# A decoder layer on one core: score products in pairs on half the array's rows, three banks of scores, heads normalised per unit, and the second set's marks moved together

## The chip, the cores and the metric

The kernel runs on one core of a Trainium2 chip. The metric is the device time of one execution in microseconds. Lower is better. The engines are TensorE (PE, with its weight loads as PEld), VectorE (DVE), ScalarE (ACT), GpSimd (POOL) and SyncE (SP). Each has its own queue of instructions that it works through in order, and they meet through semaphores.

## The reference, cut to what matters

One decoder layer over x of 2 x 1024 tokens of 256 features, all in f32:

```python
x = layernorm(x + L0_attn(x))      # keys = h@Wk+bk, exp of key_att, cumsum over tokens, times values
x = layernorm(x + L0_xattn(x))     # 16 heads of 16 features over a context of 77 rows, masked softmax
x = layernorm(x + L0_ffn(x))       # 8 experts, 256 -> 1024 -> 256, the best 2 of each token, gelu
# inside L0_xattn:
scores = einsum('bhqd,bhkd->bhqk', Q, K) / sqrt(16);  scores = where(mask, -inf, scores)
attn_w = nan_to_num(softmax(scores));  merged = einsum('bhqk,bhkd->bhqd', attn_w, V) ...;  return merged @ W_o.T
# inside L0_ffn: logits = flat @ router_w.T + router_b; top_k of 2; softmax over the two; out += y_e * weight_e
```

## The kernel before

**Attention stage.** The 2048 tokens are 16 tiles of 128 tokens, 4 tiles to a chunk, 4 chunks. The cross-attention runs in 64 steps H, four to a tile; a step handles 4 heads (a quad). Two steps make a unit u = H // 2 of 8 heads. For a step TensorE multiplies the queries (features on the 128 rows, 16 to a head) with a block-diagonal table of keys `kbd` to 128x308 scores in a bank of psum_a and adds the mask with a second, bf16 product (`scores`, lines 1690 to 1714). The table holds zeros outside the 4 heads of a quad, so only 64 of the 128 rows of a product carry something: rows 0 to 63 in even steps, 64 to 127 in odd ones. VectorE takes the maximum (`maximum`, line 1212), ScalarE the four exponentials (`exponentials`, line 924), TensorE turns the probabilities (`turn_probs`, lines 1726 and 1731; two blocks of 128 in even steps into psum_c bank 0, three in odd steps into bank 1), ScalarE evicts them (`turned_probs`, line 937), and TensorE multiplies a unit with the values (`weigh_values`, line 1745, into psum_v). Per tile follow `normalise_heads` on VectorE (lines 1199 to 1205), `turn_heads` on TensorE (line 1755, into psum_m), its eviction (943), `project_out` (1763, psum_m), `residual` on VectorE (1174), `x2_invert` on GpSimd (607), `x2_normalise` on ScalarE (968), `output_features` (1679) and the router's logits (1686).

The order on each engine is written out by hand: a loop over H in each engine's program. In TensorE's step H come turn_probs(H), scores(H + 2), in even steps weigh_values(H/2 - 1), in steps 4t + 6 turn_heads(t), then pieces of the first attention for later chunks (`turn_attention` 1655, `x1_features` and `normalised` 1618, `keys`, `key_weights`, `queries`, `values` all 1611), and in steps 4t + 7 project_out(t). Scores of step H lie in bank H % 2 of psum_a. From step 50 on the routing of the first set (tiles 0 to 6) runs beside it: marks, a table of tokens, and from step 58 the gathers of token rows (`load_tile`, line 754).

**Expert stage.** Token rows are gathered into 39 tiles of 128; for each tile t TensorE runs `up(t)` (line 1860, 64 matmuls), the turn of the next tile's rows (`turn_rows(t + 1)`, 1800), and `down(t - 1)` (1885, 16 matmuls in either of two banks). ScalarE runs `hidden(t)` (gelu, 1041), `turned_rows(t + 1)` (953), `weighed_bias(t)` (1053), in this order; weighed_bias(t) waits for the variance that VectorE's sum_row(t - 2) makes, since it reuses its buffer. VectorE runs, per iteration t, inner_norm(t - 1), outer_norm(t - 2), indices(t + 2), weigh_output(t), add_input(t), sum_row(t), and GpSimd invert(t), load_base(t + 1), gathers of tiles ahead, add_bias(t + 1), store_tile(t - 1). sum_row(t) waits for the base rows that load_base(t) gathered.

The first seven tiles (FIRST = 7) hold only tokens of the first set. For the second set (tiles 7 and on) VectorE compares numbers into marks in three passes, `mark_positions(LAST)` and `mark_columns(LAST)` (line 1407, two instructions each) and `mark_tokens(LAST)` (line 1425, two). TensorE sums them (`mark_pairs(LAST)`, 1821), VectorE writes the table (line 1578), and `map_tiles(1)` and `load_tile(7)` on GpSimd follow.

## Time and profile before

| | us |
|---|---|
| three runs | 526.98, 528.07, 531.04 (median 528.07) |
| profiled execution: its own time | 529.84 |
| its span, first to last instruction | 528.1 |
| mean granted TensorE clock | 0.983 of full speed |
| busy: TensorE matmuls, weight loads | 492.8 (93%), 441.7 (84%) |
| busy: VectorE, ScalarE, GpSimd | 359.0 (68%), 266.5 (50%), 267.6 (51%) |

The span of 528.1 us is what the views below divide; the time of the same execution is 1.7 us longer. Busy times of matmuls overlap each other, because their ends are modelled, so what one costs is read from the distance between starts. An idle time in brackets stands before the instruction that ended it, with what it waited for.

### The profile page before, as it was taken

What the parts mean: (1) busy time and instruction counts of PE and PEld (TensorE: products, weight loads), DVE (VectorE), ACT (ScalarE), POOL (GpSimd) and SP (SyncE); (2) the same over time, 40 slices, a digit from 0 to 9 for tenths busy, and PEclk for the clock granted to TensorE, in tenths of its full rate; (3) what the DMA queues carried; (4) which work ended last, traced back from release to release, by engine and by line L of the source; (5) the groups of instructions that cost most, each with busy time, mean ns of one, the idle gap of its engine ahead of it and who ended that gap; (6) DMA issues with size and microseconds to landing.
All of it is one profiled execution on the core that took longest, in us unless ns stands there. A gap on an engine that the chain in (4) does not pass through costs nothing.

```text
span 528.1 us, 10924 instructions
## 1 busy us (share of the span) xinstructions
PE 492.8 (93%) x3286; PEld 441.7 (84%) x3286; DVE 359.0 (68%) x1035; ACT 266.5 (50%) x878; POOL 267.6 (51%) x407
## 2 busy tenths in 40 slices
PE   6879999989999899899949999999999999999991
PEld 6668877878888778899939999999999999999980
DVE  4878777767668885347965557765776566766675
ACT  3856677676867577552422344434444343444330
POOL 4342342223222524146666567775776576676555
PEclk9989999999999999999979999999999999999997
DMA  8049830745565736354374555665655666666420
GB/s 235 8 137 282 267 119 3 266 135 183 174 226 177 236 100 221 123 199 142 118 274 146 192 183 200 224 226 195 198 192 220 207 232 223 202 208 232 137 63 1
DMA packets 57536, 93.84 MB, mean 178 GB/s; under 512 B 12143, under 2 KB 49273, under 8 KB 52359
## 3 DMA queue, kind: packets, MB, share of 16 engines
q1 hardware_dynamic: 50231, 80.05, 44.7%
q0 software_dynamic: 5616, 12.82, 8.3%
q8 instruction: 28, 0.46, 0.4%
q10 hardware_dynamic: 1632, 0.27, 0.3%
q14 instruction: 29, 0.24, 0.1%
HBM read 65.64 MB, written 30.32 MB: 182 GB/s over the span
## 4 chain that ended last, share of the span: by engine, by line
PE 32%; issue 19%; DVE 18%; POOL 16%; DMA 9%; ACT 4%; POOLq 2%; SPq 0%; DVEq 0%; ACTq 0%
PE psum_b L1611 6%; PE psum_a L1710 4%; DMA work<-weighed_outputs,routing 4%; PE psum_v L1745 4%; POOL routing L809 4%; POOL out L813 3%; DMA front_then_w_ring<-token_rows,routing 3%; DMA weighed_outputs<-work 2%; POOL work L805 2%; DVE routing L1478 2%; PE psum_m L1763 2%; PE psum_m L1611 2%; POOL front_then_w_ring L754 2%; POOL work L800 2%; PE psum_a L1860 1%
## 5 line engine op out<-in xcount | busy, mean ns | idle before, releaser
L1041 ACT ACTIVATE front_then_w_ring<-psum_b,front_then_w_ring 128x128 f32<-128x128 f32 x160 | 45.5, 369 | 64.0 <-PE psum_b L1860 62.7
L1041 ACT ACTIVATE front_then_w_ring<-psum_a,front_then_w_ring 128x128 f32<-128x128 f32 x152 | 43.1, 369 | 65.4 <-PE psum_a L1860 65.4
L1860 PEld LDWEIGHTS psum_b<-front_then_w_ring 128*128 128x128 f32 x640 | 74.5, 192 | 1.4 <-issue 0.5
L1860 PE MATMUL psum_b<-front_then_w_ring 128*128 128x128 f32 x640 | 75.2, 275 | 0.1
L1885 PE MATMUL psum_v<-expert_w,front_then_w_ring 128*128 x320 | 72.5, 379 | 0.0
L924 ACT ACTIVATE work<-psum_a,score_max 128x77 f32<-128x77 f32 x256 | 62.2, 335 | 19.5 <-DVE score_max L1212 19.3
L1860 PEld LDWEIGHTS psum_a<-front_then_w_ring 128*128 128x128 f32 x608 | 70.9, 192 | 0.9
L1860 PE MATMUL psum_a<-front_then_w_ring 128*128 128x128 f32 x608 | 71.2, 275 | 0.0
L1885 PE MATMUL psum_c<-expert_w,front_then_w_ring 128*128 x304 | 70.6, 386 | 0.0
L1885 PEld LDWEIGHTS psum_v<-expert_w,front_then_w_ring 128*128 128x128 f32 x320 | 59.3, 190 | 7.3
L1885 PEld LDWEIGHTS psum_c<-expert_w,front_then_w_ring 128*128 128x128 f32 x304 | 57.3, 194 | 7.5 <-issue 0.3
L809 POOL TENSOR_TENSOR routing<-routing,minus_half 128x2 f32<-128x2 f32 x38 | 28.3, 744 | 58.5 <-DVE routing L1480 58.4
L800 POOL DMA_INDIRECT work<-weighed_outputs,routing x39 | 45.0, 1153 | 16.1 <-DMA weighed_outputs<-work 8.1
L1611 PE MATMUL psum_b<-front_then_w_ring,front_weights_then_tail 128*128 128x256 f32 (+1 forms) x216 | 49.0, 372 | 2.3 <-ACT front_then_w_ring L895 2.3
L813 POOL DMA_INDIRECT out<-work,routing x39 | 40.1, 1027 | 12.8 <-issue 8.2
L1611 PEld LDWEIGHTS psum_b<-front_then_w_ring,front_weights_then_tail 128*128 128x128 f32 x216 | 37.7, 190 | 8.7 <-ACT front_then_w_ring L895 3.5
L754 POOL DMA_INDIRECT front_then_w_ring<-token_rows,routing x39 | 38.1, 976 | 11.3 <-POOL routing L752 10.5
L1484 DVE TENSOR_TENSOR work<-work 128x256 f32<-128x256 f32 x38 | 16.5, 433 | 39.7 <-DMA work<-weighed_outputs,routing 39.2
L1745 PEld LDWEIGHTS psum_v<-front_weights_then_tail,work 128*128 128x128 f32 x320 | 39.2, 191 | 4.8 <-issue 4.8
L1212 DVE TENSOR_REDUCE score_max<-psum_a 128x4 f32<-128x308 f32 x64 | 30.1, 471 | 12.8 <-PE psum_a L1713 12.3
L1745 PE MATMUL psum_v<-front_weights_then_tail,work 128*128 128x51 f32 (+2 forms) x320 | 38.7, 268 | 0.0
L1492 DVE SCALAR_TENSOR_TENSOR work<-work,routing,front_weights_then_tail 128x256 f32<-128x256 f32 x39 | 18.9, 486 | 28.6 <-POOL routing L809 28.6
(257 smaller groups left out, 881.9 us busy)
## 6 DMA issues: line engine op xcount, KB each, us to landing
front_then_w_ring<-in_w1b SPq DMA_DIRECT2D x39, 1028.0 KB
weighed_outputs<-routing SPq DMA_DIRECT2D x16, 1024.0 KB, 6.3
expert_w<-in_w SPq DMA_DIRECT2D x8, 1024.0 KB, 10.6
weighed_outputs<-work SPq DMA_DIRECT2D x37, 128.0 KB, 2.2
token_rows<-front_then_w_ring SPq DMA_DIRECT2D x16, 128.0 KB
token_rows<-routing SPq DMA_DIRECT2D x1, 1152.0 KB, 5.4
second_buffers<-in_x SPq DMA_DIRECT2D x4, 256.0 KB, 4.8
front_weights_then_tail<-in_b SPq DMA_DIRECT2D x1, 1024.0 KB, 9.0
```

Source lines behind the costliest of these rows:

```text
L754: pool.indirect_dma_start(xt[t % ROWS], None, rows_dram, bass.IndirectOffsetOnAxis(load_of[:, t % ROWS:t % ROWS + 1], 0)).then_inc(xt_in[t ...
L800: pool.indirect_dma_start(base[t % 3], None, yw_dram[0:1 + YW_COLS * P, :], bass.IndirectOffsetOnAxis(row_idx[:, t % IDX, 0:1], 0)).then_i ...
L809: pool.tensor_tensor(rstd[:, t % 4], veps[:, t % 2], mhalf[:, 0:2], ALU.pow).then_inc(rstd_out, 1)
L813: pool.indirect_dma_start(out, bass.IndirectOffsetOnAxis(row_idx[:, t % IDX, 1:2], 0), u_rows[t % 3], None, bounds_check=T - 1, oob_is_err ...
L924: last = act.activation(prob[:, u % RING_U, at_k:at_k + SC], pa[:, H % 2, g * SC:(g + 1) * SC], ACT.Exp, bias=smax[:, j % 2, head:head + 1])
L1041: last = act.activation(hidT[t % 2][:, c, :], src[:, n, q * P:(q + 1) * P], ACT.Gelu, bias=bias[:, c:c + 1])
L1212: dve.tensor_reduce(smax[:, t % 2, quad * HG:(quad + 1) * HG], pa[:, H % 2, 0:HG * SC].rearrange("p (h k) -> p h k", h=HG), AX.X, ALU.max, ...
L1611: last = pe.matmul(dst[:, c, :], w[:, k, c * P:(c + 1) * P], src[:, k, :], start=(k == 0), stop=(k == KD - 1))
L1710: pe.matmul(dst, qT[it % 2][:, half, j * P:(j + 1) * P], kbd[:, it // CPB, half, g * HG:(g + 1) * HG, :].rearrange("p h k -> p (h k)"), st ...
L1745: last = pe.matmul(pv[:, half * width + v0:half * width + v1], probT[:, u % RING_U, c, :], vblk[:, t // (CPB * CT), half, c, v0:v1], start ...
L1860: last = pe.matmul(dst[:, n, q * P:(q + 1) * P], w1[:, k, c * P:(c + 1) * P], xtT[t % 2][:, k, :], start=(k == 0), stop=(k == KD - 1))
L1885: last = pe.matmul(y_psum(t), hidT[t % 2][:, c, :], w2_v[:, bass.ds(e, 1), c, :].rearrange("p a d -> p (a d)"), start=(c == 0), stop=(c == ...
```

## The change

Scores: psum_a gets a third bank, the one that was psum_m. The bank of a step is H % 2 in steps 0 to 5 and H % 3 from 6 on. Steps 0 and 1 and all steps from 8 on are multiplied in pairs, in the even step before: first both score products, each on only the 64 rows that carry something, then both masks. Steps 2 to 7 stay single and full.

Heads: the values of a unit of 8 heads go to psum_v columns 0 to 135 for every unit, and normalise_heads runs per unit. project_out writes columns 256 to 511 of the same bank. turn_heads writes psum_c bank 0, columns 256 to 511, except for the last tile; this bank also takes the turned probabilities of even steps, so turn_heads waits for their eviction. What used psum_m otherwise uses bank 2 of psum_a. residual, x2_invert and x2_normalise come one step later.

Expert stage: VectorE runs the three mark passes of the second set one behind the other, ahead of sum_row(0). later_map and the table come in iteration 2, ahead of sum_row(2). mark_pairs(LAST) on TensorE comes behind up(4) and not up(5). GpSimd runs rows_of_choice(1) ahead of its loop, map_tiles(1) and load_tile(7) at the start of iteration 2, and then load_tile(t + 5) in every iteration.

```diff
+PAIRED = 8
+def bank(H):
+    return H % 2 if H < PAIRED - 2 else H % 3
...
+        def heads_psum(t):
+            return pc[:, 0, D:2 * D] if t < TILES - 1 else pa[:, 2, 0:D]
+        def unit_psum():
+            return pv[:, 0:HALF * VW]
+        def output_psum():
+            return pv[:, D:2 * D]
...
 # GpSimd, H loop
-                if H % QUADS == 1 and H >= 9:
-                    x2_invert((H - 9) // QUADS)
+                if H % QUADS == 2 and H >= 10:
+                    x2_invert((H - 10) // QUADS)
...
 # GpSimd, expert loop
+            rows_of_choice(1)
             for t in range(LAST_TILE):
+                if t + AHEAD == FIRST:
+                    map_tiles(1)
+                    load_tile(FIRST)
                 invert(t)
...
-                if t == 0:
-                    rows_of_choice(1)
-                if t == 2:
-                    map_tiles(1)
-                for t_l in tiles_loaded_at(t):
-                    load_tile(t_l)
+                if FIRST < t + AHEAD < SLOT_TILES:
+                    load_tile(t + AHEAD)
...
 # ScalarE, H loop
-                if H % QUADS == 2 and H >= 10:
-                    x2_normalise((H - 10) // QUADS)
+                if H % QUADS == 3 and H >= 11:
+                    x2_normalise((H - 11) // QUADS)
...
 # VectorE, H loop
-                if quad == 2 and H >= 6:
-                    normalise_heads((H - 6) // QUADS)
-                if quad == 1 and H >= 9:
-                    residual((H - 9) // QUADS)
+                if H % 2 == 0 and H >= 4:
+                    normalise_heads((H - 4) // 2)
+                if quad == 2 and H >= 10:
+                    residual((H - 10) // QUADS)
...
 # VectorE, expert stage
             add_input(1)
+            mark_positions(LAST)
+            mark_columns(LAST)
+            mark_tokens(LAST)
             sum_row(0)
             indices(3)
-            mark_positions(LAST)
             row(inner_norm(0))
             sum_row(1)
-            mark_columns(LAST)
...
                 add_input(t)
-                sum_row(t)
                 if t == 2:
-                    mark_tokens(LAST)
                     later_map()
-                if t == FIRST - 4:
                     dve.wait_ge(pos_mm, LAST + 1)
                     dve.tensor_tensor(token_of[:, 0:P], table_psum(LAST), first_token_of, ALU.add).then_inc(table_ready, 1)
+                sum_row(t)
...
 # TensorE
+            def score_product(H, rows):
+                it, h = divmod(H, STEPS)
+                j, quad = divmod(h, QUADS)
+                half, g = divmod(quad, HC // HG)
+                pe.matmul(pa[:, bank(H), 0:HG * SC], qT[it % 2][rows, half, j * P:(j + 1) * P],
+                          kbd[rows, it // CPB, half, g * HG:(g + 1) * HG, :].rearrange("p h k -> p (h k)"), start=True, stop=False)
+            def score_pair(H):
+                before_scores(H)
+                before_scores(H + 1)
+                if H == PAIRED:
+                    pe.wait_ge(kexp_ready, 4)
+                if H >= PAIRED:
+                    pe.wait_ge(exp_ready, H - 1)
+                score_product(H, slice(0, HG * DK))
+                score_product(H + 1, slice(HG * DK, 2 * HG * DK))
+                add_mask(H)
+                add_mask(H + 1)
...
             def weigh_values(u):
-                if half == 0 and t >= 1:
-                    pe.wait_ge(merged_ready, t)
+                if u >= 1:
+                    pe.wait_ge(merged_ready, u)
+                if u >= 4 and half == 0:
+                    pe.wait_ge(r2_ready, t - 1)
...
             def turn_heads(t):
-                pe.wait_ge(merged_ready, t + 1)
+                pe.wait_ge(merged_ready, 2 * t + 2)
+                if t < TILES - 1:
+                    pe.wait_ge(pT_ready, t * QUADS + 7)
+                    if t >= 2:
+                        pe.wait_ge(x2T_ready, t - 1)
...
             def project_out(t):
                 pe.wait_ge(mT_ready, t + 1)
+                pe.wait_ge(merged_ready, min(2 * t + 3, 2 * TILES))
...
             def attention_step(H):
                 turn_probs(H)
-                if H + 2 < CHUNKS * STEPS:
+                if H + 2 < PAIRED:
                     scores(H + 2)
+                elif H % 2 == 0 and H + 2 < CHUNKS * STEPS:
+                    score_pair(H + 2)
...
-                if t == FIRST - 2:
+                if t == FIRST - 3:
                     mark_pairs(LAST)
```

## Rows read from the trace of the kernel before

**Rows 1.** Stretches, columns named in the first line: attention, the hole, the expert stage.
```profile
core 0: us, PE busy (x) PEld busy (x) DVE busy (x) ACT busy (x) POOL busy (x), PEclk, DMA share, GB/s
...
60.00:100.00 40.00, 39.02 (x246) 32.53 (x245) 30.49 (x82) 29.39 (x96) 15.36 (x42) 1.00 0.40 131
...
260.00:300.00 40.00, 32.90 (x215) 30.24 (x213) 23.91 (x73) 12.83 (x43) 22.84 (x31) 0.91 0.57 187
300.00:400.00 100.00, 100.00 (x695) 94.37 (x695) 66.16 (x194) 40.66 (x135) 67.87 (x84) 1.00 0.62 210
```

**Rows 2.** TensorE's timeline (start us, us, what) inside an attention step.
```profile
162.90 0.69 PE L1710 MATMUL psum_a<-front_weights_then_tail,front_then_w_ring 128*128 128x308 f32 x2
163.42 0.30 PE L1713 MATMUL psum_a<-identity_per_head,mask_bias 77*128 77x308 bf16 x1
163.56 1.89 PE L1611 MATMUL psum_b<-front_then_w_ring,front_weights_then_tail 128*128 128x256 f32 x8
```

**Rows 3.** Groups on tile psum_a: count, duration ns min/median/max, first and last start.
```profile
L1710 PEld LDWEIGHTS psum_a<-front_weights_then_tail,front_then_w_ring x64: 186/192/337, 25.4 to 174.0; 128*128 128x128 f32 x64
L1710 PE MATMUL psum_a<-front_weights_then_tail,front_then_w_ring x64: 422/425/721, 25.4 to 174.3; 128*128 128x308 f32 x64
```

**Rows 4.** Timeline of all engines around turn_heads of step 10.
```profile
65.18 0.42 PE L1755 MATMUL psum_m<-identity,work 128*128 128x128 f32 x2
...
66.55 0.94 ACT L924 ACTIVATE work<-psum_a,score_max 128x77 f32<-128x77 f32 x4
...
67.38 0.39 ACT L937 ACTIVATE work<-psum_c 128x256 f32<-128x256 f32 x1
...
67.55 0.55 PE L1731 MATMUL psum_c<-identity,work 128*128 128x128 f32 x3 [0.22 <-ACT work L924]
```

**Rows 5.** The same around turn_heads of step 62.
```profile
215.66 0.41 PE L1755 MATMUL psum_m<-identity,work 128*128 128x128 f32 x2
215.71 0.41 ACT L937 ACTIVATE work<-psum_c 128x256 f32<-128x256 f32 x1
```

**Rows 6.** VectorE groups by shape: normalise_heads (busy us, mean ns).
```profile
L1205 DVE TENSOR_TENSOR work<-psum_v,prob_scale 128x256 f32<-128x256 f32 x16 | 6.8, 425 | 0.6
...
L1199 DVE RECIPROCAL prob_sum_recip<-psum_v 128x16 f32<-128x16 f32 x16 | 4.0, 250 | 3.1 <-PE psum_v L1745 3.1
...
L1202 DVE SCALAR_TENSOR_TENSOR prob_scale<-score_max,prob_sum_recip 128x16 f32<-128x16 f32 x16 | 3.4, 211 | 0.5
```

**Rows 7.** TensorE's timeline: up(4), around down(4), and at the hole.
```profile
247.86 3.81 PE L1860 MATMUL psum_b<-front_then_w_ring 128*128 128x128 f32 x32
...
260.14 0.39 PE L1800 MATMUL psum_m<-identity,front_then_w_ring 128*128 128x128 f32 x2
260.36 3.62 PE L1885 MATMUL psum_v<-expert_w,front_then_w_ring 128*128 x16
...
274.66 0.69 PE L1800 MATMUL psum_m<-identity,front_then_w_ring 128*128 128x128 f32 x2 [7.10 <-DMA front_then_w_ring<-token_rows,routing]
275.22 5.19 PE L1885 MATMUL psum_c<-expert_w,front_then_w_ring 128*128 x16
```

**Rows 8.** VectorE's timeline: the first marks of the second set, and the table.
```profile
245.34 1.42 DVE L1407 TENSOR_TENSOR second_buffers<-routing 128x1152 f16<-128x1152 f16 x2
...
265.57 0.28 DVE L1578 TENSOR_TENSOR routing<-psum_c,routing 128x128 f32<-128x128 f32 x1
```

**Rows 9.** The chain of waits (start us, us, what): the gather of tile 7.
```profile
269.88 4.73 DMA front_then_w_ring<-token_rows,routing
```

**Rows 10.** ScalarE's timeline: weighed_bias(2) and turned_rows(4).
```profile
244.92 0.51 ACT L1053 ACTIVATE work<-front_weights_then_tail,routing 128x256 f32 x1 [6.61 <-DVE routing L1480]
...
247.34 0.43 ACT L953 ACTIVATE front_then_w_ring<-psum_m 128x256 f32<-128x256 f32 x1
```

**Rows 11.** Stretches again: the clock after sparse work.
```profile
24.00:27.00 3.00, 2.53 (x12) 1.80 (x12) 2.38 (x12) 0.85 (x3) 1.62 (x3) 0.78 0.16 15
27.00:30.00 3.00, 3.00 (x11) 2.24 (x11) 1.66 (x6) 0.97 (x4) 0.00 (x0) 0.66 0.12 14
```

More of the change, by code:

```diff
@@ L370, in decoder_layer @@
         v_rows = R[0:SC, 3840:3840 + B * D].rearrange("p (b u h d) -> p b u h d", b=B, u=2, h=HALF)
[L372 removed]
+        pa = ctx.enter_context(nc.psum_tensor("psum_a", [P, 3, 512], F32))
         pb = ctx.enter_context(nc.psum_tensor("psum_b", [P, KD, 512], F32))
@@ L923, in exponentials @@
                     at_k = (head % HALF) * SC
-                    last = act.activation(prob[:, u % RING_U, at_k:at_k + SC], pa[:, H % 2, g * SC:(g + 1) * SC], ACT.Exp,
+                    last = act.activation(prob[:, u % RING_U, at_k:at_k + SC], pa[:, bank(H), g * SC:(g + 1) * SC], ACT.Exp,
                                           bias=smax[:, j % 2, head:head + 1])
@@ L1688, in route_logits, with before_scores @@
                 last.then_inc(lg_mm, 1)
-            def scores(H):
-                it, h = divmod(H, STEPS)
-                j, quad = divmod(h, QUADS)
-                half, g = divmod(quad, HC // HG)
+            def before_scores(H):
                 if H == CPB * STEPS:
@@ L1739, in weigh_values @@
                     pe.wait_ge(own_made, 3 + 2 * B)
-                if half == 0 and t >= 1:
-                    pe.wait_ge(merged_ready, t)
-                width = HALF * VW
+                if u >= 1:
+                    pe.wait_ge(merged_ready, u)
+                if u >= 4 and half == 0:
+                    pe.wait_ge(r2_ready, t - 1)
+                if u == 2 * TILES - 1:
+                    pe.wait_ge(r2_ready, TILES - 1)
                 for c in range(BLOCKS):
-                    v0, v1 = (0, width) if c == 0 else (BLOCK_HEADS[c][0] * VW, (BLOCK_HEADS[c][-1] + 1) * VW)
-                    last = pe.matmul(pv[:, half * width + v0:half * width + v1], probT[:, u % RING_U, c, :],
+                    v0, v1 = (0, HALF * VW) if c == 0 else (BLOCK_HEADS[c][0] * VW, (BLOCK_HEADS[c][-1] + 1) * VW)
+                    last = pe.matmul(unit_psum()[:, v0:v1], probT[:, u % RING_U, c, :],
                                      vblk[:, t // (CPB * CT), half, c, v0:v1], start=(c == 0), stop=(c == BLOCKS - 1))
@@ L1762, in project_out @@
                 for k in range(KD):
-                    last = pe.matmul(pm[:, D:2 * D], mergedT[:, t % 2, k, :], wo_s[:, k, :], start=(k == 0), stop=(k == KD - 1))
+                    last = pe.matmul(output_psum(), mergedT[:, t % 2, k, :], wo_s[:, k, :], start=(k == 0), stop=(k == KD - 1))
                 last.then_inc(o_mm, 1)
@@ L1838, in _ @@
             queries(0)
-            scores(0)
-            scores(1)
+            score_pair(0)
             turn_attention(1)
```

74 lines of the change are left out of this document (33 added, 41 removed).

## The prediction

> **What bounds the kernel now.** I read the table of stretches first: which engine is full in which stage. In the attention stage (roughly 27 to 217 us) TensorE is busy for 39.0 of the 40 us shown, VectorE for 30.5 and ScalarE for 29.4 [rows 1]. In the expert stage TensorE is full, 100 of 100 us, except in one stretch, 260 to 300, where 7.1 us are missing and the granted clock averages 0.91 [rows 1]. So a microsecond of TensorE work removed from attention is worth up to a microsecond, and so is the hole at 267 us; work on the other engines counts only where TensorE waits for it. Second, TensorE's timeline inside a step, read by start times, since the busy times overlap: a score product of 128x308 in f32 is two matmuls that occupy the array for 0.52 us, and the next work starts 0.14 after the mask product [rows 2]. Third, the groups on psum_a: one score matmul lasts 425 ns while they start some 260 apart, so 0.16 us is the tail that an isolated one would show [rows 3]. Fourth, the hole: TensorE's timeline for its place, then VectorE's, ScalarE's and the chain of waits for its cause; their rows come with that step.
>
> **Score products in pairs.** Each of the 64 steps has two score matmuls, 128 in all (64 of them in the form shown, 64 in a twin form) [rows 3]. Now 29 pairs (steps 0 and 1, then 8 to 63) are issued as A1 A2 on rows 0 to 63, B1 B2 on rows 64 to 127. No row of this trace shows two matmuls on different halves, so I bound it. If nothing overlaps, the gain is 0. If both passes of B lie beside those of A, it is 2 x 0.26 = 0.52 a pair, 15.1 us in all. A1 and A2 need the same rows and stay serial; if the issue order is kept, only B1 can lie beside A2: three passes instead of four, 0.26 a pair, 29 x 0.26 = 7.5 us. I take this one. The Trainium skill, "TensorE: Matmul & The Clock Gate", Part 3, says that matmuls start and end in program order and that those of different row groups start about 4 ns apart; by that rule the saving is the same three passes. Going from 128 rows to 64 and back may cost something at each of 2 x 29 = 58 places. The nearest row is the 77-row mask product between full products: it starts 0.52 after the first score pass and the next work 0.14 later, so that change of rows costs nothing [rows 2]. I take 0 and keep as the upper end a switch that lets the array run empty and uncovers a load of weights (below). The even scores' mask now follows both products, some 0.26 to 0.52 us later; the maximum and the exponentials of that step have two steps to hide it. The odd scores come a step earlier, which only relieves VectorE and ScalarE.
>
> **Turned heads in another bank.** turn_heads (15 times in the loop) now writes the bank that holds the turned probabilities, so it waits until ScalarE has evicted those of the same step (line 937). That wait is new, and behind it on TensorE queue the pieces of the next chunk and the odd step's transposes and products. At step 10 TensorE turned the heads at 65.18, ScalarE finished the eviction at 67.38 + 0.39, and a signal takes some 0.06: 2.65 us late [rows 4]. At the last place, step 62, it is 0.52 [rows 5]. Over all 15 places the same subtraction gives 11 positive waits, these being the first and the last, 9.25 us together; that is the upper bound. Relief: at step 10 ScalarE's x2 normalisation stood ahead of the exponentials and held them back until 66.55, though their maximum was there near 65.0; it moves behind them, which makes 1.4 us [rows 4]. The pair puts some 0.4 us more product work between the even transposes and turn_heads, at each of the 11 waits; and at three of them TensorE idled anyway before the odd transposes, 0.22 at the one shown [rows 4], 1.65 together. 9.25 - 1.4 - 11 x 0.3 - 1.65 = 2.9; I take +3, with 0 and 9 as ends.
>
> **Smaller moves, each taken as 0.** Heads are normalised in 32 halves instead of 16 wholes: 16 x (0.25 + 0.21 + 0.42) = 14 us becomes, with nearly fixed reciprocals and a product of half the width, about 20 [rows 6]. VectorE's spare quarter of attention hides the 6 us; weigh_values now waits for the half before, but that is done right behind the maximum, ahead of the exponentials that TensorE needs first anyway. If VectorE were the bound, it would cost those 6. residual and x2_invert move one step later; the work is the same and its readers moved too. Before the first gather (load_tile(0)) they now stand in the same step, about 1.4 us more ahead of it, but the 1 MB bias load that competes with it moves behind it as well. TensorE idles 1.44 there today; -1.4 to +1.5, taken 0. project_out shares the bank with the units; its new wait is for work that follows a maximum issued two steps ahead: 0.
>
> **Second set's marks in a row.** Today TensorE ends up(6) at 267.5 and idles 7.10 until the rows of tile 7 land; then the clock is at its lower level (1.2 GHz): the turn takes 0.69 instead of 0.39, down(5) 5.19 instead of 3.62. Hole: 7.1 + 0.3 + 1.6 = 9.0 [rows 7]. The table is written at 265.57 + 0.28, the last act of iteration 3 [rows 8]; the gather behind it is issued at 269.88 and takes 4.73 [rows 9]. Now map and table stand in iteration 2. The price: three marks (1.42 us of busy time, 1.33 by their starts, 4.0 in all [rows 8]) stand ahead of sum_row(0). ScalarE's weighed_bias(2) waits for exactly that, already 6.61 us today, and hidden(3) and turned_rows(4) queue behind it; the turned rows end at 247.77 and up(4) starts at 247.86, without slack [rows 7, 10]. So a new hole of 4.0 us opens before up(4). Following it: up(4) at 251.9, table at about 262 (the base rows of tile 1, asked for 4 us later, hold VectorE), gather at 263.4, landed at 268.1; TensorE reaches tile 7 at 271.4. The old hole closes. In the 4.0 us the clock probably falls, too: after the sparse work near 24 us it was 0.78 and 0.66 for two stretches of 3 us, 3.4 us at the lower level [rows 11], worth up to 1.7. I take 1.6. Sum: -9.0 + 4.0 + 1.6 = -3.4; ends -5.1 (the clock stays) and 0 (tile 7 or the next two come late again, 3.4 us).
>
> **Sum.** -7.5 + 3.0 - 3.4 = -7.9 us. The profiled execution took 529.84 (span 528.1), 1.8 above the median of 528.07; against the median: **520.2 us**.
>
> **Rivals.**
> 1. *Switching rows costs more than the overlap gives (slower).* Place: the 58 borders in attention, on TensorE. If at each the array runs empty (425 - 260 = 0.16 us [rows 3]) and the next weights can't be loaded ahead (0.19 by the weight-load row [rows 3]), it is 58 x 0.35 = 20.5 us: 540.7. With the empty array alone, 9.4 us: 529.6. It decides from 7.9 / 58 = 0.14 us a border. For it: nothing in this trace has 64 rows, so nothing speaks against it but the mask's free border. The Trainium skill, "TensorEngine Tiling (Array Packing)", Key Properties, says that a change of tiling mode drains TensorE, and gives no price; no row here shows whether 77 rows count as another mode. Chance 0.18 for the cheap form, 0.14 for the dear one.
> 2. *No overlap at all*, the change doesn't do what it says: -7.9 + 7.5 = -0.4, 527.7. Every f32 matmul is already a pass of a full-width stream. Chance 0.12.
> 3. *Full overlap of both passes*: -15.5, 512.6. It needs B1 to start with A1. Chance 0.06.
> 4. *The wait for the eviction of the turned probabilities takes it back*: +9 instead of +3, and VectorE's 6 us partly with it: 526 to 529. For it: the attention stage leaves TensorE no slack, and the longest waits were VectorE's doing, which gets more work. Chance 0.10.
> The forecast has 0.40.
>
> **How the numbers follow.** About 1% (5.3 us) can be told from no change. Faster by more than that (below 522.8): forecast and rival 3, 0.46. Within 1%: the cheap form of 1 (0.18), 2 and 4, together 0.40, less 0.04 that may fall above 533.4: 0.36. Slower: 0.14 + 0.04 = 0.18. The range leaves out the dear switch (0.14) and the outer part of full overlap: 512.5 to 533. The forecast's own range, from its ends of the eviction wait, the hole and the gather: 516 to 528.
>
> **What would show it.** On TensorE the second product's first matmul starts within a few ns of the first product's second; from the first of the pair to the mask 0.78 us means three passes, 0.52 full overlap, 1.04 none. A gap before the pair and before the mask prices the border. turn_heads would wait for line 937's successor, 3 us in all. A wait of 4.0 us before up(4), none before tile 7, and the clock low once between 248 and 256. The forecast is wrong if attention is not 4 us shorter, or the stretch from down(2) to up(7) not 3 us shorter.

## The result: slower by 3.7 per cent, and the profile after

The changed kernel took **549.54 us** in the median (545.59 to 550.61, 4 runs), against 528.05 before; the ratio is 1.0368, interval 1.0314 to 1.0421. That is 19 us slower (21.5 by the medians), outside the range of 512.5 to 533 and on the other side of the forecast. The profiled execution has a span of 547.4 us, 19.3 more than before. Because the kernels of different groups below ran beside their own runs of the kernel before, I compare them by their ratios, and turn a ratio into microseconds with 528.

First the stretches, columns as in [rows 1].

```profile
core 0: us, PE busy (x) PEld busy (x) DVE busy (x) ACT busy (x) POOL busy (x), PEclk, DMA share, GB/s
60.00:100.00 40.00, 35.88 (x234) 28.84 (x234) 30.12 (x84) 28.54 (x92) 14.86 (x40) 1.00 0.31 98
...
190.00:220.00 30.00, 26.27 (x143) 19.94 (x143) 17.89 (x73) 17.60 (x63) 8.57 (x18) 0.78 0.50 179
...
300.00:400.00 100.00, 100.00 (x692) 94.43 (x692) 67.30 (x196) 42.08 (x141) 67.94 (x85) 1.00 0.62 210
```

The expert stage is as it was. In attention TensorE is busy for 35.9 of 40 us where it was 39.0 [rows 1], no other engine does more in the same time, and late in the stage the granted clock falls to 0.78. Attention lost more than the whole kernel did: the last projection starts at 248.3 us instead of 225.7, 22.6 later, and the expert stage gave 3.3 back.

Waiting is only a part of this. Of the 22.6 us, the waits that the profile lists (below) make 13.2. Over the same stretch, from 27 us to the last projection, TensorE's busy time rose too, from 188.9 to 197.5 us, although the pairs took work away, and the granted clock was 0.94 where it was 0.99. If TensorE had been bound by its clock all the time, that would be worth 0.05 x 221 = 11 us, an estimate from above.

The pair saves what was forecast, but not in the way that was forecast. TensorE's timeline in a step, as [rows 2]:

```profile
142.24 0.38 PE L1753 MATMUL psum_c<-identity,work 128*128 128x128 f32 x2
142.55 0.79 PE L1716 MATMUL psum_a<-front_weights_then_tail,front_then_w_ring 64*128 64x308 f32 x4
143.27 0.44 PE L1722 MATMUL psum_a<-identity_per_head,mask_bias 77*128 77x308 bf16 x2
143.55 1.10 PE L1775 MATMUL psum_v<-front_weights_then_tail,work 128*128 128x136 f32 x9
```

From the first product to the first mask 0.72 us (forecast 0.78 for three passes, 1.04 for none saved), and 1.00 to the next work. Two single products with their masks took 2 x (0.52 + 0.14) = 1.32 [rows 2]. But there are no three passes one behind the other. Two views of short windows, 142.5 to 142.6 and 143.1 to 143.2, part the four matmuls of that line into two and two:

```profile
142.55 0.53 PE L1716 MATMUL psum_a<-front_weights_then_tail,front_then_w_ring 64*128 64x308 f32 x2
...
142.92 0.43 PE L1716 MATMUL psum_a<-front_weights_then_tail,front_then_w_ring 64*128 64x308 f32 x2
```

Two matmuls start within 0.01 us of each other, the other two 0.36 later, again within 0.01, and the mask 0.36 behind those. The two passes of one product start some 0.26 apart in the kernel before [rows 3], so I read a couple as one pass of the even and one of the odd product, although no row names which. Then both passes lie side by side, as rival 3 had it, but a couple takes 0.36 us instead of 0.26; why, no run shows.

The same place with full rows (e2 below):

```profile
143.98 0.38 PE L1753 MATMUL psum_c<-identity,work 128*128 128x128 f32 x2
144.20 1.20 PE L1716 MATMUL psum_a<-front_weights_then_tail,front_then_w_ring 128*128 128x308 f32 x4
145.24 0.43 PE L1722 MATMUL psum_a<-identity_per_head,mask_bias 77*128 77x308 bf16 x2
```

Behind the same two transposes the half-row pair starts 0.31 us after them, the full-row pair 0.22: the border from 128 to 64 rows costs 0.09 us here, and 0.07 behind the router's logits (0.44 against 0.37), at nearly every pair of both kernels. From the transposes to the mask it is 1.03 against 1.26 us, from the logits to the mask 1.16 against 1.49. So the half rows save 0.23 us a pair in one half of the pairs and 0.33 in the other, about 7.5 us in the 28 pairs of the loop.

What TensorE waits for between 27 and 240 us (releaser, us in total, times, longest), before and after:

```profile
PE psum_c L1726 <- ACT work L924: 3.3, 3, 1.5
PE psum_c L1731 <- ACT work L924: 1.7, 3, 0.8
PE psum_b L1800 <- DMA front_then_w_ring<-token_rows,routing: 1.4, 1, 1.4
```

```profile
PE psum_c L1788 <- issue: 5.6, 6, 1.6
PE psum_b L1662 <- DVE front_then_w_ring L1157: 3.2, 3, 1.6
PE psum_b L1618 <- ACT front_then_w_ring L901: 2.3, 3, 1.6
PE psum_v L1797 <- ACT work L949: 2.1, 5, 0.9
PE psum_b L1618 <- ACT front_then_w_ring L888: 2.0, 4, 0.6
PE psum_c L1788 <- ACT work L943: 1.6, 1, 1.6
PE psum_c L1788 <- DVE work L1212: 1.3, 1, 1.3
```

All lines of these lists together are 9.8 us before and 23.0 after. The turned heads (L1788) wait for 8.5 of them, where they waited for none; 1.3 of the 8.5 are put down to VectorE's normalisation (L1212) and not to the eviction. "issue" stands where the profile names no single releaser; the timeline of all engines around one of these waits does (step 54, with the residual's sum first, and one pass of the first set's marks behind it):

```profile
212.03 0.41 DVE L1180 TENSOR_TENSOR front_then_w_ring<-psum_v,front_then_w_ring 128x256 f32<-128x256 f32 x1
...
213.22 1.15 DVE L1414 TENSOR_TENSOR front_weights_then_tail<-routing 128x896 f16<-128x896 f16 x2
214.29 0.47 DVE L1219 TENSOR_REDUCE score_max<-psum_a 128x4 f32<-128x308 f32 x1
...
214.80 0.97 ACT L930 ACTIVATE work<-psum_a,score_max 128x77 f32<-128x77 f32 x4 [2.57 <-DVE score_max L1219]
...
215.64 0.40 ACT L943 ACTIVATE work<-psum_c 128x256 f32<-128x256 f32 x1
...
216.14 0.41 PE L1788 MATMUL psum_c<-identity,work 128*128 128x128 f32 x2 [1.35 <-issue]
...
217.03 0.79 PE L1797 MATMUL psum_v<-front_weights_then_tail,work 128*128 128x256 f32 x1 [0.16 <-ACT work L949]
```

VectorE comes to the odd maximum at 214.29 only, behind the residual of the tile with its moments (0.8 us) and, at this place, 1.15 us of marks that the kernel before has too. ScalarE's exponentials wait for it, the eviction of the turned even probabilities stands behind them on ScalarE's queue, and the turned heads start 0.1 us after that eviction ends. It is the chain that the prediction named, at the upper end of its price.

The expert stage after, as [rows 7], down(2), up(4), the turn of tile 5 and down(3):

```profile
266.69 3.62 PE L1920 MATMUL psum_v<-expert_w,front_then_w_ring 128*128 x16
274.82 5.44 PE L1895 MATMUL psum_b<-front_then_w_ring 128*128 128x128 f32 x32 [4.51 <-issue]
...
281.10 0.39 PE L1836 MATMUL psum_a<-identity,front_then_w_ring 128*128 128x128 f32 x2
281.33 3.62 PE L1920 MATMUL psum_c<-expert_w,front_then_w_ring 128*128 x16
```

There is the new hole ahead of up(4), 4.51 us (forecast 4.0), and none of over 0.2 us behind it.

### The profile page after: what moved, and what is told of

Read it like the earlier page. It is cut to its first block, busy times and chain, and to the rows that moved or that the text cites. A ratio compares the mean times of both kernels' runs of the same rounds, so it can differ in the third digit from the quotient of the medians.

```text
span 547.4 us, 11002 instructions
## 1 busy us (share of the span) xinstructions
PE 500.5 (91%) x3286; PEld 441.9 (81%) x3286; DVE 365.0 (67%) x1083; ACT 267.2 (49%) x878; POOL 269.6 (49%) x407
## 4 chain that ended last, share of the span: by engine, by line
PE 33%; issue 19%; POOL 17%; DVE 14%; DMA 10%; ACT 5%; POOLq 1%; SPq 0%; DVEq 0%; ACTq 0%
DMA work<-weighed_outputs,routing 9%; PE psum_b L1618 8%; PE psum_v L1775 5%; POOL routing L815 4%; PE psum_a L1716 4%; POOL out L819 3%; POOL work L811 2%; PE psum_v L1797 2%; POOL work L806 2%; DVE routing L1485 2%; PE psum_a L1722 2%; PE psum_a L1618 2%; ACT work L930 2%; POOL front_then_w_ring L769 2%; DMA weighed_outputs<-work 1%
## 5 line engine op out<-in xcount | busy, mean ns | idle before, releaser
L1895 PE MATMUL psum_b<-front_then_w_ring 128*128 128x128 f32 x640 | 77.2, 280 | 4.5 <-issue 4.5
L1895 PEld LDWEIGHTS psum_b<-front_then_w_ring 128*128 128x128 f32 x640 | 76.7, 197 | 5.7 <-issue 4.9
L1920 PE MATMUL psum_c<-expert_w,front_then_w_ring 128*128 x304 | 69.0, 380 | 0.0
L1618 PE MATMUL psum_b<-front_then_w_ring,front_weights_then_tail 128*128 128x256 f32 (+1 forms) x216 | 52.5, 392 | 5.9 <-ACT front_then_w_ring L901 3.5
L1618 PEld LDWEIGHTS psum_b<-front_then_w_ring,front_weights_then_tail 128*128 128x128 f32 x216 | 40.0, 203 | 12.9 <-ACT front_then_w_ring L901 5.1
L1775 PEld LDWEIGHTS psum_v<-front_weights_then_tail,work 128*128 128x128 f32 x320 | 40.3, 196 | 1.9 <-ACT work L943 0.6
L622 POOL TENSOR_SCALAR routing<-routing 128x1 f32<-128x1 f32 x14 | 5.1, 361 | 71.7 <-DVE routing L1186 71.7
```

What stands on the lines that cost most here:

```text
L1618: last = pe.matmul(dst[:, c, :], w[:, k, c * P:(c + 1) * P], src[:, k, :], start=(k == 0), stop=(k == KD - 1))
L1775: last = pe.matmul(unit_psum()[:, v0:v1], probT[:, u % RING_U, c, :], vblk[:, t // (CPB * CT), half, c, v0:v1], start=(c == 0), stop=(c == ...
L1895: last = pe.matmul(dst[:, n, q * P:(q + 1) * P], w1[:, k, c * P:(c + 1) * P], xtT[t % 2][:, k, :], start=(k == 0), stop=(k == KD - 1))
L1920: last = pe.matmul(y_psum(t), hidT[t % 2][:, c, :], w2_v[:, bass.ds(e, 1), c, :].rearrange("p a d -> p (a d)"), start=(c == 0), stop=(c == ...
```

## The experiments

The theory after the result: the time is lost in attention to two handovers that lost their cover, the eviction ahead of the turned heads, and ScalarE's work between steps that have both score products and steps that have none. Rivals: the row halves (borders), the lower clock, VectorE's extra instructions.

| kernel | median us | ratio to before | interval |
|---|---|---|---|
| changed | 549.54 | 1.0368 | 1.0314 to 1.0421 |
| e1 expert edits alone | 527.05 | 0.9973 | 0.9951 to 0.9995 |
| e2 pairs, all 128 rows | 548.56 | 1.0393 | 1.0327 to 1.0459 |
| e3 single scores | 537.36 | 1.0177 | 1.0120 to 1.0233 |
| e4 e3, heads in their own bank | 528.98 | 1.0009 | 0.9982 to 1.0035 |
| e5 changed, eviction first | 540.64 | 1.0236 | 1.0183 to 1.0288 |
| e6 e5, projection later | 554.86 | 1.0551 | 1.0480 to 1.0622 |
| e7 e3, eviction first | 531.61 | 1.0060 | 1.0028 to 1.0093 |
| e8 e5, residual earlier | 545.06 | 1.0336 | 1.0291 to 1.0380 |
| e9 e5, pair in the odd step | 536.67 | 1.0143 | 1.0088 to 1.0199 |
| e10 e5, all 128 rows | 545.47 | 1.0305 | 1.0244 to 1.0367 |
| e11 e5, more products | 541.16 | 1.0227 | 1.0174 to 1.0279 |
| e12 e9, heads in the odd step | 537.16 | 1.0134 | 1.0100 to 1.0169 |
| e13 e1, one bias later | 526.38 | 0.9896 | 0.9856 to 0.9936 |
| e14 e1, all biases later | 524.89 | 0.9910 | 0.9875 to 0.9944 |

**Which part costs: e1 to e4.** e1 is the kernel before with the diff of the expert stage alone. e2:

```diff
-                score_product(H, slice(0, HG * DK))
-                score_product(H + 1, slice(HG * DK, 2 * HG * DK))
+                score_product(H, slice(0, P))
+                score_product(H + 1, slice(0, P))
```

e3 takes the changed kernel and issues scores(H + 2) in every step again, in bank H % 2; e4 moreover frees the heads:

```diff
-            return pc[:, 0, D:2 * D] if t < TILES - 1 else pa[:, 2, 0:D]
+            return pa[:, 2, 0:D]
...
-                    pe.wait_ge(pT_ready, t * QUADS + 7)
```

> The kernel before with only the expert-stage edits (marks in a row, table and first gather of the second set in iteration 2, mark_pairs behind up(4)). The prediction's term for it is -3.4 us: 524.6 against 528.0. If these edits carry part of the loss, it is above 528; if they carry more of a gain than the term, below 523.

> The changed kernel with the same pairs, banks and waits, but each score product of a pair over all 128 rows, so nothing can overlap. Theory (the waits on turned heads and on what follows them make the loss, the pairs do save 0.23 us each): about 6 us slower than the changed kernel, 556. Rival (going from 128 to 64 rows and back costs more than it gives, or the row halves disturb the neighbours): faster than the changed kernel, 535 to 545.

> The changed kernel with single, full scores in two banks issued each step as before; the heads still go to the bank of the turned probabilities with the wait for their eviction, normalised per unit, output product beside the units. Theory (that wait): as slow as the changed kernel or slower, 548 to 558. Rival (the pairing and its order, even scores later, is what starves VectorE and ScalarE): 526 to 532.

> As the single-score variant, but the turned heads go to a bank of their own and wait only for the merged heads, as before. It keeps the normalisation per unit, the output product in the units' bank, residual and x2 one step later, and the expert edits. Theory (the wait for the eviction): back to 524 to 530. Rival (the shared bank of units and output product, or the later residual, makes the loss): above 540.

The steps between them: expert edits -1.4 us; e4 over e1 +1.9 (normalisation in halves, the shared bank, the residual a step later; the intervals overlap, so it may be nothing); the turned heads in the shared bank with their wait for the eviction, e3 over e4, **+8.9**; both scores in the even step, with a third bank, e2 over e3, **+11.4**; the row halves, changed over e2, -1.3, within the intervals of each other. So the row halves are no loss, and the 7.5 us of work that they save buy next to nothing.

e4 came as expected and e1 between its term and no change. e2 and e3 fit neither of their cases: e2 was to be 6 us slower than the changed kernel and is not, and e3 lies between its ranges, since the wait and the pairing each carry about half of the loss.

Where did the saved 7.5 us go? Not into waits: those listed are 23.0 us in the changed kernel and 22.1 in e2. The granted clock differs: 0.94 in the changed kernel from 27 us to its last projection, 0.98 in e2, and over the whole span 0.960 to 0.972 in the four runs of the one, 0.973 to 0.981 in the four of the other. A clock lower by 0.04 over 220 us is worth up to 9 us, an estimate, which is about what the shorter products save. That TensorE is granted less because it has less to do fits this, and e11 below; no run shows it as the cause.

**The eviction wait alone: e5 and e7.** One order turned round on ScalarE, in pairs (e5) and with single scores (e7):

```diff
-                if H >= 2:
+                early = H % QUADS == 3 and H >= 7
+                if early:
+                    turned_probs(H - 1)
+                if H >= 2:
                     exponentials(H)
-                if H >= 1:
+                if H >= 1 and not early:
                     turned_probs(H - 1)
```

> The changed kernel with one order turned round on ScalarE: in the last step of each tile (4t+7) the eviction of the turned even probabilities (0.40 us) goes before the exponentials of the odd scores (0.97 us), not behind them. Theory handover: TensorE's turning of the heads waits for that eviction, which ScalarE gives only after exponentials that themselves wait for the odd maximum on VectorE; then the waits of the turned heads (7.2 us between 60 and 222 us, against nothing in the kernel before) shrink to under 1 us and the time falls by 6 to 9 us, to 541 to 543. Rival ScalarE: the exponentials start later by as much as the eviction comes earlier, the next turned odd probabilities are late by the same, and the time stays at 547 to 550. Rival order: the loss sits in the pair itself (both scores in the even step), then only 2 to 4 us come back.

> The kernel with single full-row scores (that of e3, 537.4 us) with the same turn of order on ScalarE as e5. Theory handover: the 8.4 us between e3 and e4 are this wait alone, and this kernel comes to 528.5 to 531. Rival ScalarE: 536 to 538, the wait only moves. Rival bank: the heads in the bank of the turned probabilities cost in other ways too, then 532 to 535.

-7.0 us in pairs, -6.2 with single scores: for the most part the turned heads waited for the order of two instructions on ScalarE. e7 ends at 531.6, just above the range of its theory and 2.7 us above e4 by the ratios; that rest of the shared bank's 8.9 us is not this order. With the wait nearly gone from both, pairs with full rows (e10, below) still stand 13 us above the single scores (e7).

**What is left of the pair's price: e6, e8, e9, e12.** e6 moves the projection to step 4t+8 behind the next pair; e8 moves the residual to step 4t+9 and lets the weighing wait for it; e9 moves the pair:

```diff
-                elif H % 2 == 0 and H + 2 < CHUNKS * STEPS:
+                elif H % 2 == 1 and H + 3 < CHUNKS * STEPS:
                     score_pair(H + 2)
```

(with logits and ranks a step later); e12 turns the heads behind turn_probs(4t+7), ahead of that pair, and has the old order on ScalarE.

> e5 and beside it the output projection of tile t in step 4t+8 behind the next pair of scores, not at the end of step 4t+7. Theory bare odd steps: with both score products in the even step, nothing stands between the turned heads and the projection in the odd step but the turned odd probabilities (0.5 us), and TensorE waits for ScalarE's copy of the turned heads (6.8 us in all in the full-row kernel with pairs, 0.4 us with single scores); with the pair (1.1 us) as cover these waits go and the kernel is 4 to 7 us faster than e5, 535 to 538. Rival: the projection is hidden behind ScalarE anyway and the time is that of e5 within 2 us. Rival later residual: the projection comes later, so the residual and the next weighing wait, and it is slower than e5 by 3 us or more.

> e5 and beside it the residual of tile t one step earlier on VectorE (step 4t+9, behind the odd maximum, where the kernel before has it), with the weighing of the next unit waiting for it. Theory odd maximum: the odd maximum stands behind normalisation and residual (1.3 us) on VectorE and the odd exponentials wait for it; freed of the residual the kernel is 2 to 5 us faster than e5, 537 to 541. Rival: the weighing (1.2 us) now waits for the residual on TensorE and the kernel is slower than e5 by 2 to 8 us, 545 to 550.

> e5 with the pair of score products moved from the even to the odd step: at odd step H the scores of H+2 and H+3 on the two row halves (steps up to 8 single, the last one single); the logits of a tile and the ranks go one step later, into the bank of an odd step. Theory bare odd steps: in e5 the even step holds pair (1.1 us), weighing (1.2 us) and turned heads, the odd step nothing but the turned probabilities and what waits for ScalarE (projection and pieces: 12 us of waits against 3 in e7); with pair and weighing in different steps the waits go and the kernel comes to 525 to 532, 9 to 15 us below e5. Rival early scores: what costs is that the even score of a pair is made late against its maximum and exponentials, whichever step it is in, or that queries are not ready a step earlier; then it stays at 538 to 545. Rival clock: the time follows the stretches at the lower clock; the granted clock of 60 to 222 us then tells more than the waits.

> e9 (pair in the odd step, 536.7 us) with the turned heads moved into the odd step too, behind the turned odd probabilities and ahead of the pair, and ScalarE's eviction back behind the exponentials. The odd step then holds turned probabilities 0.5, heads 0.4, pair 1.1 and projection 1.0, and the pair stands between heads and projection. Theory cover: neither the eviction nor the copy of the heads is waited for (3.1 us of waits in e9), 531 to 535. Rival balance: the even step has only 1.6 us of work and TensorE waits longer for the odd exponentials (5.9 us in e9), 537 to 541. If it is 535 to 537, both do and undo each other.

e6 and e8 went the way of a rival in time, but not for its reason: waits for the residual are 0.5 us in e6 and 0.7 in e8. e6 shows best what happened. TensorE's and ScalarE's timeline of it, from the odd step to the next even one:

```profile
205.29 0.49 PE L1761 MATMUL psum_c<-identity,work 128*128 128x128 f32 x3
205.49 0.39 ACT L949 ACTIVATE work<-psum_c 128x256 f32<-128x256 f32 x1 [1.21 <-PE psum_c L1791]
205.78 0.59 ACT L974 ACTIVATE front_then_w_ring<-front_then_w_ring,routing 128x256 f32<-128x256 f32 x1
206.26 0.96 ACT L930 ACTIVATE work<-psum_a,score_max 128x77 f32<-128x77 f32 x4
207.28 0.44 PE L1689 MATMUL psum_c<-identity,front_then_w_ring 128*128 128x128 f32 x2 [1.50 <-ACT work L930]
```

With the projection gone, the odd step has only its transposes (0.49 us) to cover 0.96 us of exponentials and the way there: ScalarE stood idle for 1.21 us until the heads were turned, copied them and normalised the tile, and only then came to the exponentials. TensorE waits for them, 13.3 us at 12 places, and e6 is 17 us slower than e5 (14 by the medians), far more than I had expected even on its rival's side. The bare step was real, but the projection had been its cover. In e8 the new waits are for the even exponentials (4.2 us at 3 places). It is 5 us slower, but all its listed waits together are no longer than those of e5 (18.7 and 19.3 us), so its cause stays open.

e9 puts the pair where nothing else stood. TensorE's waits between 27 and 240 us in e9:

```profile
PE psum_c L1762 <- ACT work L930: 5.9, 7, 1.9
PE psum_b L1665 <- DVE front_then_w_ring L1160: 2.7, 2, 1.9
PE psum_b L1840 <- DMA front_then_w_ring<-token_rows,routing: 1.9, 2, 1.1
```

The waits for the copy of the turned heads (1.3 us at 4 places in e5) and for the eviction in line 888 ahead of the pieces (2.0 us at 4 places) are gone; 4.9 us come back, half of what I expected, and the time lies between the ranges of theory and rival. In their place the odd transposes wait for their exponentials (5.9 us), since now the even step is the thin one. e12 moves 0.4 us of work more into the odd step: these waits grow to 8.6 us, the others shrink, and the time is the same. By the ratio (535.1 us) that is the third case of its expectation, by the median (537.16) the lower end of its rival's.

**Half rows once the wait is gone: e10.** e5 with the edit of e2.

> e5 with both products of a pair over all 128 rows (the zero rows too), as e2 is to the changed kernel. It costs TensorE 0.23 us in each of 28 pairs, 6.4 us of work. Theory cover: TensorE has waits of about 15 us between 27 and 240 us in e5 and takes the longer products in them; 540 to 543. Rival TensorE bound: 546 to 548, the half rows save their whole work once the eviction wait is gone.

3.6 us slower than e5 by the ratios (4.8 by the medians), between the two theories. The intervals overlap, so this is likely and not shown: the shorter products pay a part of what they save. What keeps the rest is again not the listed waits (19.3 us in e5, 19.7 in e10); the granted clock of 60 to 240 us is 0.95 in e5 and 0.98 in e10.

**The clock: e11.**

```diff
+                if H % QUADS == 3 and H >= 11:
+                    for _ in range(3):
+                        pe.matmul(pa[:, bank(H), 0:P], ident[:, :], ident[:, :], start=True, stop=True)
                 if H % QUADS == 3 and H >= 7:
                     project_out((H - 7) // QUADS)
```

> e5 with three more 128x128 products (about 0.2 us each at the higher clock, results thrown away) on TensorE ahead of each projection from tile 1 on, where TensorE waits for ScalarE's copy of the turned heads. 14 times 0.6 us is 8.4 us more work. Theory clock: the lower-clock stretches of e5 (mean granted clock 0.966 over the span against 0.984 in e4) come of the idle time; filled, the clock is over 0.975 and the time falls by 2 to 5 us, to 535 to 538. Theory cover: the fill takes waits for half of its length and delays by the rest, 543 to 546, clock or not.

The stretch of 60 to 240 us, e5 first, e11 below it:

```profile
60.00:240.00 180.00, 162.41 (x1045) 130.95 (x1044) 119.97 (x374) 117.00 (x387) 55.44 (x119) 0.95 0.44 146
```

```profile
60.00:240.00 180.00, 165.41 (x1152) 136.83 (x1151) 121.66 (x380) 118.27 (x391) 55.36 (x119) 1.00 0.46 151
```

```profile
220.62 0.83 PE L1829 MATMUL psum_a<-identity 128*128 128x128 f32 x6
221.29 1.03 PE L1800 MATMUL psum_v<-front_weights_then_tail,work 128*128 128x256 f32 x4
```

Three products take 0.67 us, 9 us in 14 places, and cost nothing: 541.2 against 540.6. The granted clock went from 0.95 to 1.00, so a mean of 0.95 over 180 us, 18 us of them at 1.2 GHz, was there and went. Neither theory's number came out. The waits that the added work fills pay little of it: 1.3 us of waits for the copied heads are gone, but all listed waits together fell by 0.7 only (19.3 to 18.6). 18 us at half the clock cost up to 9 us, an estimate, so the clock paid for most of the 9 us. These are the two profiled executions; over all four runs of each the granted clock of the span was 0.966 to 0.977 in e5 and 0.973 to 0.986 in e11. Keeping the clock at 2.4 GHz in this way gives no net gain. And the price of the pairs doesn't need the clock: e10 at 0.98 (56 to 243 us) stands 13 us above e7 at 0.99 (56 to 231.5 us).

**The expert stage: e1 read closer, e13, e14.** TensorE of e1 first, then its ScalarE:

```profile
244.31 3.62 PE L1875 MATMUL psum_v<-expert_w,front_then_w_ring 128*128 x16
252.45 6.50 PE L1850 MATMUL psum_b<-front_then_w_ring 128*128 128x128 f32 x32 [4.51 <-issue]
```

```profile
249.50 0.51 ACT L1044 ACTIVATE work<-front_weights_then_tail,routing 128x256 f32 x1 [11.02 <-DVE routing L1471]
249.92 2.15 ACT L1032 ACTIVATE front_then_w_ring<-psum_a,front_then_w_ring 128x128 f32<-128x128 f32 x8
251.92 0.43 ACT L944 ACTIVATE front_then_w_ring<-psum_m 128x256 f32<-128x256 f32 x1
```

ScalarE's bias of slot tile 2 waits for VectorE, and behind it queue the hidden layer of tile 3 (ready long before) and the turned rows of tile 4, for which TensorE waits. up(4) itself takes 6.50 us instead of 3.73. The order on ScalarE is that of the kernel before [rows 10]. e13 moves this bias alone, behind turned_rows(4):

```diff
             weighed_bias(1)
-            weighed_bias(2)
...
+                if t == 3:
+                    weighed_bias(2)
                 weighed_bias(t)
```

e14 moves every bias one tile on:

```diff
             weighed_bias(1)
-            weighed_bias(2)
...
-                weighed_bias(t)
+                weighed_bias(t - 1)
+                if t == SLOT_TILES - 1:
+                    weighed_bias(t)
```

> e1 (the kernel before with the expert-stage edits alone, 527.1 us) with one move on ScalarE: the weighed bias of slot tile 2, which waits for VectorE's variance of tile 1 until 249.2 us, goes behind the hidden layer of tile 3 and the turned rows of tile 4. Theory order: the hole of 4.5 us ahead of the up products of tile 4 is this wait, and the clock that falls after it costs 2.8 us more (6.50 against 3.73 us). Both go, less a new wait for the bias of tile 3 (until 255.8 us) of some 2.5 us ahead of tile 5 and its clock: 521 to 524. Rival VectorE: the marks on VectorE (1152-wide, 4.5 us) are the bound and the hole only moves one tile on whole: 526 to 528. Rival clock: the hole goes but the clock falls at the next one, 524 to 526.

> e13's move for every slot tile: the weighed bias of tile t-1 behind the hidden layer of tile t and the turned rows of tile t+1. Theory order: the later holes go too and it is as fast as e13 or up to 3 us faster, 519 to 523. Rival: VectorE gets each bias later and weighs the outputs later, the down products wait for it at 17 tiles, and it is slower than e13 by 2 us or more.

Both are faster than the kernel before by about 1%: **they beat both kernels of this study.** Against e1 they gain 4.1 and 3.3 us by the ratios, as theory order has it, but only 0.7 and 2.2 by the medians: e13's median of 526.4 lies in the range of rival VectorE. What speaks for the order is e13's trace. The hole ahead of up(4) is gone, and one of 2.51 us stands ahead of up(5), as expected, not the whole 4.5. In e14 no such hole is left; in its profiled execution (527.18 us, one of the slower of its twelve) TensorE is early enough to wait for the gathers again:

```profile
266.76 0.44 PE L1791 MATMUL psum_m<-identity,front_then_w_ring 128*128 128x128 f32 x2 [1.19 <-DMA front_then_w_ring<-token_rows,routing]
...
278.84 0.44 PE L1791 MATMUL psum_m<-identity,front_then_w_ring 128*128 128x128 f32 x2 [4.23 <-DMA front_then_w_ring<-token_rows,routing]
279.41 5.40 PE L1876 MATMUL psum_v<-expert_w,front_then_w_ring 128*128 x16
```

So e14 isn't told from e13: what it saves on ScalarE, the DMA takes in this execution. Whether it does in the faster ones no trace shows.

## Why the prediction was wrong

1. **Pairing, -7.5 taken.** As TensorE work the size is right: about 7.5 us net in 28 pairs. The picture behind it is not. The forecast had three passes of 0.26 and no border; the rows show two couples of 0.36 and a border of 0.07 to 0.09, so the match of the sums is luck. What made the prediction wrong is the worth of it: +11.4 us for putting both products into one step (e2 over e3) and -1.3 for their shorter rows. The failed sentence is "the maximum and the exponentials of that step have two steps to hide it. The odd scores come a step earlier, which only relieves VectorE and ScalarE". I asked who waits for the scores, and not what the score product of the odd step had covered. It was 0.66 us of work between the turned heads and their copy, between a piece's products and their eviction, between one set of exponentials and the next. Nowhere in the sum is there a term for that.
2. **Border 0, rivals 1 and 2.** The border is not free, but small: 0.07 to 0.09 us ahead of each pair, some 2 us in all, and what there may be ahead of the mask lies within the second couple's 0.36, where rival 1 had 0.16 or 0.35 at 58 places. The times alone rule out its dear form only: 20.5 us of borders less 7.5 saved would make the changed kernel 13 us slower than e2, and it is 1.3 faster. The cheap form, 9.4 less 7.5, would lie within the noise of that difference; the rows rule it out. That the sign of the result is rival 1's is chance.
3. **The eviction wait, +3 taken, ends 0 and 9.** Mechanism right, size at its end: 8.5 us of waits after (1.3 of them for VectorE), 8.9 between e3 and e4, 7.0 given back by e5. The reliefs that I subtracted did not come. At step 10 the prediction had ScalarE's exponentials held back by the x2 normalisation alone, and gave 1.4 us for its leaving. Ahead of it stood the normalisation of x1, 1.09 us, and it still does after:

```profile
65.35 1.09 ACT L964 ACTIVATE second_buffers<-second_buffers,ln_shift,ln_rstd 128x256 f32<-128x256 f32 x2 [0.75 <-POOL ln_shift L638]
66.35 0.94 ACT L930 ACTIVATE work<-psum_a,score_max 128x77 f32<-128x77 f32 x4
```

   The exponentials start at 66.35 instead of 66.55 [rows 4], 0.2 us earlier and not 1.4, and TensorE waits for 1.64 us there. The 0.4 us of longer pair work ahead of the heads is taken up where the odd maximum is late (2.57 us of waiting on ScalarE at 214.80), and the residual, a step later, now stands ahead of that very maximum. Rival 4 had this, at 526 to 529, but with -7.5 for the pair still in it.
4. **Smaller moves, 0 taken.** e4 over e1: +1.9 us, so nearly right. The price of the halves is as costed. VectorE's normalisation after, as [rows 6]:

```profile
L1212 DVE TENSOR_TENSOR work<-psum_v,prob_scale 128x128 f32<-128x128 f32 x32 | 9.3, 291 | 1.1
L1206 DVE RECIPROCAL prob_sum_recip<-psum_v 128x8 f32<-128x8 f32 x32 | 6.5, 205 | 11.9 <-PE psum_v L1775 11.7
L1209 DVE SCALAR_TENSOR_TENSOR prob_scale<-score_max,prob_sum_recip 128x8 f32<-128x8 f32 x32 | 6.4, 200 | 1.1
```

   22.2 us instead of 14, where about 20 were forecast; hidden but for those 1.9 at most.
5. **Expert stage, -3.4 taken.** e1 measures -1.4, and -2.3 by the spans (525.8 against 528.1). Its terms: hole ahead of tile 7 closed as forecast (-9.0), the new hole 4.5 instead of 4.0, and the clock behind it 6.50 - 3.73 = 2.8 instead of 1.6. That makes -1.7. The step that failed is the clock's: I priced what falls within the hole, but the lower clock outlasted it and slowed the up products behind it. In the changed kernel the same stage gave 3.3, since there up(4) took 5.44.

The sum with measured terms: +11.4 - 1.3 + 8.9 + 1.9 - 1.4 = 19.5 us, against 19.4 by the ratio; that it closes is no finding, since the five are differences along one chain of kernels. What the pairing costs is seen best between e10 and e7, 13 us apart with little of the eviction wait in either (0.6 and 1.2 us): TensorE waits 4.5 us against 1.0 ahead of the projection, and 4.6 against 0 for ScalarE's evictions ahead of the pieces (56 to 243 us). All listed waits together differ by 6.5 us. Another 5 us lie in TensorE's busy time, 170.5 us in 56 to 243 of e10 and 165.5 in 56 to 231.5 of e7, for which no row names a cause; they stay open, and that e9 got only 4.9 us back by another place says the same.

## What to carry to other kernels

Ahead of merging work from two steps into one, ask of each piece what it has been covering where it stands: on a queue that runs in order, an instruction that feeds a slow engine and one that reads its result need something between them, and a cheaper pair in one place can leave the other place bare. A wait that looks like one engine's slowness can be the order of two short instructions on it (0.40 us ahead of 0.97 us gave 7 us back; one bias moved back gave 4 by the ratios, 0.7 by the medians). Work taken off an engine that also waits can buy little: 7.5 us less bought some 1.3 here, at a lower granted clock. Where a new wait has ends of 0 and 9 and every relief depends on other engines being early, take it near its upper end.

## What the runs showed of the hardware

- Two f32 products on rows 0 to 63 and 64 to 127, issued one behind the other, ran as two couples of matmuls: the two of a couple started within 0.01 us of each other, and a couple took 0.36 us. From the first to the next product that was 0.72 us where the same two products over 128 rows, four matmuls 0.26 apart, took 1.04 (144.20 to 145.24 in e2).
- Going from 128 to 64 rows cost 0.07 to 0.09 us ahead of each pair; from the 77 rows of the first mask to the next product over 128 rows it was 0.27 us, against 0.26 in e2.
- 9 us of discarded products in 14 places raised the granted clock of 60 to 240 us from 0.95 to 1.00 in the profiled executions and left the time unchanged, though the listed waits fell by 0.7 us only.
- With some 7.5 us less product work the granted clock was lower, 0.94 against 0.98 in attention (changed kernel and e2, listed waits 23.0 and 22.1 us), and the time fell by 1.3 us only, within the intervals.
- After a wait of 4.51 us, 32 products of 3.73 us took 6.50 in e1 and 5.44 in the changed kernel (granted clock 0.56 and 0.69 over them, so 1.2 and 2.4 GHz mixed); after 2.51 us in e13 they took 5.44 as well. The price of a hole lies partly behind it, and it doesn't follow the hole's length alone.
